# A four-head graph attention layer with 0/1 masks: exact waits and a hinted loop, the normalisation on ScalarE, and the accumulator banks emptied one step later

## The reference, cut to what matters

```python
# x: 8192 x 256 f32; adj: 8192 x 8192 int32, 0 or 1, about 0.2% ones; W: 4 heads x 256 x 64; a: 4 x 128
xt  = einsum('ni,hio->hno', x, W)
src = einsum('hnf,hf->hn', xt, a[:, :64]);  dst = einsum('hnf,hf->hn', xt, a[:, 64:])
e   = leaky_relu(src[:, :, None] + dst[:, None, :], 0.2)
e   = where(adj > 0, e, -inf)
h   = einsum('hij,hjf->hif', softmax(e, axis=2), xt)
out = layernorm(x + h.transpose(1, 0, 2).reshape(n, 256))      # over the 256 features, eps 1e-5
```

## Time and profile before

| | |
|---|---|
| time, 3 runs | median 2429.58 us (2426.62 to 2431.9) |
| profiled execution | 2433.28 us; its span in the trace 2431.5 us |
| PE busy | 2128.5 us, 88% |
| DVE busy | 2161.1 us, 89% |
| ACT busy | 1993.6 us, 82% |
| POOL busy | 90.7 us, 4% |
| DMA | 470.18 MB, mean 193 GB/s |
| granted TensorE clock, mean | 0.949 |

### The profile page before, as it was taken

One profiled execution on the slowest core, in us unless ns is written; L12 is line 12 of the kernel. 1 busy time (PEld: TensorE's weight loads), 2 busy tenths in 40 slices (PEclk: granted clock), 3 DMA queues, 4 the chain that ended last, 5 costly groups with the idle time before them and its releaser, 6 DMA issues. The chain is left out here.

```text
span 2431.5 us, 79550 instructions
## 1 busy us (share of the span) xinstructions
PE 2128.5 (88%) x34180; PEld 2093.7 (86%) x34180; DVE 2161.1 (89%) x2398; ACT 1993.6 (82%) x1981; POOL 90.7 (4%) x72
## 2 busy tenths in 40 slices
PE   7604999999999899998999999998989999999996
PEld 6503989998999899998999999998989988999996
DVE  4597999999889999999999999989999998988776
ACT  2235889888888898888889888888888988899995
POOL 0062000000000000000000000000000000000000
PEclk9856999999999999999999999999999999999998
DMA  8648776666555666666656666656556566623220
GB/s 300 208 188 316 256 245 228 231 210 226 182 187 188 222 215 193 194 193 216 196 186 202 212 211 195 195 194 222 190 189 205 187 223 193 193 82 111 77 55 19
DMA packets 236613, 470.18 MB, mean 193 GB/s; under 512 B 14656, under 2 KB 23104, under 8 KB 236224
## 3 DMA queue, kind: packets, MB, share of 16 engines
q1 hardware_dynamic: 231600, 447.53, 56.3%
q0 software_dynamic: 4352, 16.78, 2.0%
q10 hardware_dynamic: 272, 0.13, 0.0%
HBM read 438.83 MB, written 25.56 MB: 191 GB/s over the span
## 5 line engine op out<-in xcount | busy, mean ns | idle before, releaser
L385 ACT ACTIVATE big<-big,d_all 128x1024 int8<-128x1024 f32 x1792 | 1889.5, 1137 | 164.9 <-PE acc L747 162.0
L747 PE MATMUL acc<-big 128*128 128x130 f16 x32768 | 1955.0, 222 | 40.2 <-DVE big L549 20.2
L747 PEld LDWEIGHTS acc<-big 128*128 128x128 fp8e5 x32768 | 1929.7, 99 | 55.0 <-issue 50.9
L543 DVE SCALAR_TENSOR_TENSOR big<-big,AT 128x1024 uint32<-128x1024 uint32 x512 | 626.5, 1224 | 157.5 <-ACT big L385 118.6
L549 DVE SCALAR_TENSOR_TENSOR big<-AT,big 128x1024 uint32<-128x1024 uint32 x512 | 624.3, 1219 | 26.2 <-DVE big L543 0.5
L712 PE MATMUL tp<-ident,nat 128*128 128x128 f32 x1024 | 165.4, 287 | 227.3 <-DVE nat L464 109.2
L712 PEld LDWEIGHTS tp<-ident,nat 128*128 128x128 f32 x1024 | 114.4, 146 | 235.5 <-issue 232.3
L535 DVE TENSOR_SCALAR big<-big,d_all 128x1024 uint8<-128x1024 f32 x256 | 190.2, 743 | 0.0
L464 DVE TENSOR_SCALAR nat<-raw 128x2048 fp8e4<-128x2048 int32 x128 | 176.3, 1381 | 6.8 <-DMA raw<-in_adj_dram 6.8
L466 DVE TENSOR_SCALAR nat<-raw 128x2048 uint8<-128x2048 int32 x128 | 177.0, 1383 | 0.0
L479 DVE SCALAR_TENSOR_TENSOR AT<-AT,tp 128x512 uint32<-128x512 uint32 x224 | 152.8, 682 | 0.2
(11 more groups left out here) (46 smaller groups left out, 342.8 us busy)
## 6 DMA issues: line engine op xcount, KB each, us to landing
raw<-in_adj_dram SPq DMA_DIRECT2D x256, 1024.0 KB, 6.2
big<-v_parts SPq DMA_DIRECT2D x512, 260.0 KB, 3.5
v_parts<-big SPq DMA_DIRECT2D x16, 1040.0 KB, 4.2
big<-s_rows SPq DMA_DIRECT2D x32, 512.0 KB, 4.7
AT<-in_x_dram SPq DMA_DIRECT2D x16, 512.0 KB, 4.0
big<-in_x_dram POOLq DMA_DIRECT2D x8, 1024.0 KB, 8.5
out_dram<-big POOLq DMA_DIRECT2D x8, 1024.0 KB, 6.9
big<-in_L_gnn_W_dram SPq DMA_DIRECT2D x2, 128.0 KB, 2.6
```

The source lines that it names most:

```text
L385: ins = nc.scalar.activation(sgn[:, g % NB, b, :], srow[:, h % 2, :], ACT.Sign, bias=dflat[:, r:r + 1], scale=-1.0)
L543: nc.vector.scalar_tensor_tensor(out=word(sgn, g % NB), in0=word(sgn, g % NB), scalar=EDGE[plane], in1=edges(g), op0=ALU.bitwise_and, op1= ...
L747: return nc.tensor.matmul(acc[:, k, o:o + 2 * VO], m[:, g % NB, b, t * P:(t + 1) * P], Vr[:, v:v + 2 * VO], start=opens, stop=False, skip_ ...
```

## The change

Five edits. (1) TensorE's two pass loops carry a hint for their closing branch. (2) ScalarE's `low` moves from behind step 1 to inside step 2: one part after the second, third and fourth block of signs each. VectorE's `high` of all three parts moves from step 1 (part 0 between the two mask operations, the others behind them) to behind step 2's `rest_of` and `convert`; weighing and the rest follow one step later each. (3) VectorE compares the block for the next odd step behind the masks of the step before it, instead of ahead of that step's own masks; `keep` stands between pos and neg. (4) The wait on `AT` counts only the merges into the step's own tile. (5) Normalisation goes to ScalarE, steps 12 to 15 of the first pass of a chunk, two row tiles each, and at the very end; GpSimd makes the shift that it needs, with two more small operations.

```diff
-            def signs(n, g, h):
-                act.wait_ge(sums_done, n + 1)
-                for b in range(scalar_blocks(g)):
...
+            def normalise(c, ts):
+                act.wait_ge(shift_done, 2 * c + 2)
+                for t in ts:
+                    nc.scalar.activation(y[:, t, :], y[:, t, :], ACT.Identity, bias=shift[:, t:t + 1],
+                                         scale=rstd[:, t:t + 1]).then_inc(norm_done, 1)
...
                     for g in range(NG):
-                        signs(p * NG + g, g, h)
-                        if g == 1 and not (first and h == 0):
-                            for part in range(3):
-                                low(p - 1, part)
+                        act.wait_ge(sums_done, p * NG + g + 1)
+                        for b in range(scalar_blocks(g)):
+                            ins = sign(g, h, b)
+                            if b == scalar_blocks(g) - 1:
+                                ins.then_inc(sgn_done, 1)
+                            if g == 2 and b > 0 and not (first and h == 0):
+                                low(p - 1, b - 1)
+                        if g in (12, 13, 14, 15) and h == 0 and not first:
+                            normalise(c - 1, (2 * g - 24, 2 * g - 23))
...
-                        if scalar_blocks(g) < B:
-                            compares(n, g, h)
+                        masks_of(n, g, plane, c * H * HALF + h * HALF + (g + 1) // 2, last[g])
+                        if g < NG - 1:
+                            if scalar_blocks(g + 1) < B:
+                                compares(n + 1, g + 1, h)
...
-                        if ended and g == 1:
-                            high(p, 0)
+                        if g == 2:
+                            rest_of(n, g, plane, last[g])
                         for k in made_at(first, s):
...
-                        rest_of(n, g, plane)
+                        if g != 2:
+                            rest_of(n, g, plane, last[g])
                         if ended:
-                            if g == 1:
-                                high(p, 1)
-                                high(p, 2)
                             if g == 2:
+                                for part in range(3):
+                                    high(p, part)
+                            if g == 3:
                                 weigh(p, ec, eh)
...
-            with pe.Fori(H, NP - H) as p:
+            with nc.Fori(H, NP - H, engines=PE, hint_back_edge=True) as p:
                 one_pass(p, lambda g: [((p + H) * HALF + g // 2, g // 2)] if g % 2 == 0 else [])
-            with pe.Fori(NP - H, NP) as p:
+            with nc.Fori(NP - H, NP, engines=PE, hint_back_edge=True) as p:
                 one_pass(p, lambda g: [])
```

More of the change, by code:

```diff
@@ L17, in gat_residual_norm @@
     AX = mybir.AxisListType
+    PE = [mybir.EngineType.PE]
     RMAX = bass.bass_isa.ReduceOp.max
@@ L65, in gat_residual_norm @@
         half = sb("half", [P, T], fp32)
+        shift = sb("shift", [P, T], fp32)
         big = sb("big", [P, 24144], fp32)
@@ L147, in gat_residual_norm @@
         pow_done = sem("pow_done")
+        shift_done = sem("shift_done")
         norm_done = sem("norm_done")
@@ L326, in deviation @@
                 nc.gpsimd.tensor_tensor(out=rstd[:, :], in0=rstd[:, :], in1=half[:, :], op=ALU.pow).then_inc(pow_done, 1)
+                nc.gpsimd.tensor_scalar(shift[:, :], mv[:, :, 0], -1.0, None, ALU.mult).then_inc(shift_done, 1)
+                pool.wait_ge(pow_done, 2 * c + 2)
+                pool.wait_ge(shift_done, 2 * c + 1)
+                nc.gpsimd.tensor_tensor(out=shift[:, :], in0=shift[:, :], in1=rstd[:, :], op=ALU.mult).then_inc(shift_done, 1)
             def store(c):
@@ L379, in _, with sign @@
                     nc.scalar.activation(V_part(n, 2), rows_of(U2[n]), ACT.Copy, scale=1.0 / LOW).then_inc(hi_done, 1)
-            def signs(n, g, h):
-                act.wait_ge(sums_done, n + 1)
-                for b in range(scalar_blocks(g)):
[L384 to L387, removed]
+            def sign(g, h, b):
+                r = (g * B + b) * H + h
+                return nc.scalar.activation(sgn[:, g % NB, b, :], srow[:, h % 2, :], ACT.Sign,
+                                            bias=dflat[:, r:r + 1], scale=-1.0)
             def low(p, part):
@@ L418, in _ @@
                 low(NP - 1, part)
+            normalise(NC - 1, range(T))
         @block.vector
@@ L471, in keep @@
                 if not fresh:
-                    dve.wait_ge(neg_done, n - (g - u // 2 - 1) % NG + 4)
+                    z = (g - u // 2) % NG
+                    dve.wait_ge(pos_done if z == 0 else neg_done, n + 1 if z == 0 else n - z + 5)
                 to = AT[:, u // 2, :, u % 2, :]
@@ L544, in masks_of, with rest_of @@
                                                op0=ALU.bitwise_and, op1=ALU.bitwise_and).then_inc(pos_done, 1)
-            def rest_of(n, g, plane):
+            def rest_of(n, g, plane, kept):
+                dve.wait_ge(at_done, kept)
                 dve.wait_ge(sums_done, n + 1)
@@ L602, in spread @@
                 ins.then_inc(mv_done, 1)
[L604 to L608, removed]
             def chunk(c, plane, first=False, after_first=False, more=True):
-                kept = NG + 2 if first else UN * (c + 1) + 2 - sum(
-                    len(kept_at(False, after_first, z)) for z in range(3))
+                last = [UN * c + 2 * g + 4 for g in range(NG)]
                 for h in range(H):
@@ L626, in chunk @@
                                 keep(UN * (c + 1) + k, k + UN, plane, first, n, g)
-                                kept = kept + 1
+                                last[(k + UN) // 2] = UN * (c + 1) + k + 3
                             elif more:
                                 keep(UN * (c + 1) + k, k, 1 - plane, False, n, g)
-                                kept = kept + 1
-                        masks_of(n, g, plane, c * (NP // NC) * HALF + h * HALF + (g + 1) // 2 + 0, kept)
-                        if ended and g == 1:
-                            high(p, 0)
+                                last[k // 2] = UN * (c + 1) + k + 3
+                        if g == 2:
+                            rest_of(n, g, plane, last[g])
                         for k in made_at(first, s):
@@ L660, in chunk @@
                                 spread(c - 1)
[L661 to L664, removed]
             chunk(0, 0, first=True)
@@ L681, in _ @@
             spread(NC - 1)
-            normalise(NC - 1, range(T))
         @block.tensor
```

8 lines of the change are left out of this document (4 added, 4 removed).

## The result

The changed kernel takes 2542.05 us (median of 4 runs, 2541.64 to 2542.39) against 2428.1 us (4 runs, 2426.59 to 2431.9): ratio 1.0467, 95% interval 1.0449 to 1.0485. It is slower, as forecast, but by more: 2509 was forecast, with a range up to 2535. The profiled execution took 2542.08 us, its span 2540.5.

The account below looks back on a forecast made before the run. TensorE was bound by its closing-branch stops, with late banks behind. Ordinary passes +24.0, chunks' first passes +23.5, passes 1 to 3 +13.6, last four +16.8, end +2: +80 on 2433.3 gives 2513, as median 2509; range 2460 to 2535 us.

Parts of the forecast that it names:

- The banks: End of a pass: TensorE waits for the first `high`; an ordinary pass becomes 70.13 us, +1.41, 17 passes +24.0.
- S(14): What step 2's signs wait for at a pass's end; all issued by TensorE at T - 3.64.
- T: The moment at which TensorE would issue the next pass without any stop; the forecast's times count from it, in us.
- The hint hidden: Closing branch of TensorE's pass loop: its stop, 4.80 us, hinted or not, is hidden in the wait for the banks.
- Rival B: Pass ends: banks free as early as now, T + 2.78, with the branch gone; 2354 us; chance 0.12.
- VectorE's relief: VectorE's pass gets shorter; worth nothing where banks hold TensorE, but the 2.7 us of a chunk's first passes go.
- Passes 1 to 3: Early passes: 71.2 us each after, +2.6 for each of two; with pass 1, +13.6 together.
- Normalisation on ScalarE: First pass of a chunk: 4.0 us work plus 2.4 us wait make ScalarE 5.1 us late; 75.2 us a pass; +23.5.
- S(6): Step 6's counterpart of S(14); the shift was estimated to end some 14.2 us after it is done.
- lateness: How late ScalarE comes to step 2's signs in a chunk's first pass: 5.1 us, bounds 2.5 to 8.6.
- rival C: Pass ends: the longer stop costs more clock, 0.3 us by slope, 0.9 at worst, over 30 ends; 2536 us; chance 0.08.
- Rival A: Banks as forecast but ScalarE not late: shift ready, normalisations find room, 7 x 5 us go; 2474 us; chance 0.24.

Follow-up runs that it names:

- Experiment 7: Changed kernel with the three high parts ahead of step 2's conversion instead of behind it: 2500.88 us, ratio 1.0274.
- Experiment 4: Changed kernel with the low and high parts (emptying the banks) back in step 1, as in the kernel before: 2366.88 us, ratio 0.9728.
- Experiment 1: Changed kernel with TensorE's two pass loops unhinted, as before; all else stays: 2536.67 us, ratio 1.0426.
- experiment 2: Kernel before with nothing but the hint on TensorE's two pass loops: 2363.71 us, ratio 0.9709.
- 9: The kernel of experiment 8 with TensorE's two pass loops unhinted: 2394.3 us, ratio 0.9842.
- experiment 8: Changed kernel with the banks emptied in step 1 and normalisation on VectorE, both as before; hint, exact waits and early compares stay: 2314.51 us, ratio 0.9504.
- Experiment 5: Changed kernel with the negated mean (L330) made by VectorE instead of GpSimd: 2515.17 us, ratio 1.0326.
- Experiment 6: Changed kernel with ScalarE's normalisation in steps 14 and 15, four row tiles each, instead of steps 12 to 15: 2499.28 us, ratio 1.0262.

## Why the prediction was right in direction and too small

*The banks: right.* The chain from S(14) to the first `high` was forecast to let TensorE start at T + 6.65 and is at T + 6.45. An ordinary pass was forecast at 70.13 us and is 70.06. Experiment 7 takes one link out of the chain and gets its length back at the ends. Experiment 4 removes the delay, and the 175 us show how much the banks cost against a kernel in which they hold TensorE at almost no ordinary end. Against the kernel before it is far less, because its 4.64 us stop hid most of it.

*The hint hidden: right.* Experiment 1 shows it worthless in the changed kernel; experiments 2 and 9 show it worth 68 and 80 us where the banks are free in time. Rival B (the banks free as early as before) describes experiment 2: 2354, of which 16 are VectorE's relief, which that kernel doesn't have, so 2370; measured 2364, with restarts at T + 2.3 in most ordinary passes.

*VectorE's relief worth nothing there: in accord with the waits, not tested alone.* VectorE waits 320.9 us for signs. Where the banks are free in time, the relief shows: experiment 8 is 49 us under the hint alone. The three edits in it (early compares, `keep` between the masks, exact waits) were not taken apart.

*Passes 1 to 3: right.* 71.2 forecast; 372.35, 443.26 and 514.74 are the restarts, 70.9 and 71.5 apart.

*Normalisation on ScalarE: this term failed.* The step reads: "GpSimd adds 2.23 and two small operations." and, from it, "I estimate a wait of 2.4 us (0 to 3.6)." The wait is 6.92. The places were right: GpSimd starts 12.2 us after S(6) is done (2006.27 against 1994.1), where the forecast had about 11.5, and ScalarE is through at the same moment, where it had 11.9. The eight operations were right too (4.0 forecast, 4.04 measured; 588 ns one). Wrong was the price of GpSimd's operations. I took them at what they cost at the kernel's end, from the earlier trace rows, where VectorE is idle. In the middle VectorE works without a pause, and four operations take 6.9 us: 2.92 for the one that takes 0.25 alone. Experiment 5 removes it, and 27 us go. The kernel before already had a small sign of it: its L324 takes 0.53 us in the middle (at 1930.07) and 0.24 at the end.

In this pass L327, L330 and L333 each end within 0.11 us behind the end of a VectorE instruction (L560, L482, L567), so they look held by it. The Trainium skill, "SBUF — State Buffer", section "Who interferes with whom", states that a GpSimd instruction that reads SBUF and a VectorE instruction with two SBUF inputs, or one in a two-port mode, exclude each other for a whole instruction; these ends agree with it. Two things it doesn't settle here: L330 started beside L560 and lasted through two more of VectorE's instructions, the compare and the conversion, and the reciprocal root took its 1.68 us beside L567 and L560 as it does alone. No run varied what VectorE does beside GpSimd, so the cause behind the longer operations is argued, not shown.

*What that did to the sum.* With 6.92 for the wait, the forecast's own sum gives a lateness of 21.84 + 4.04 + 6.92 - 23.16 = 9.6 us in place of 5.1. The first passes of a chunk took 79.9 us on average instead of 75.2: 28 us more for passes 4, 8, ... 24, and 2.7 more for pass 28, where the forecast had no wait and 3.25 us came. For the profiled execution 2513 was forecast and 2542.1 measured, so these two make up the 29 us, with small differences between the other terms. The other 4 of the 33 us are no mechanism: 3.7 were taken off because the profiled execution of the kernel before lay above its median, and that of the changed kernel doesn't. The bound of 3.6 on the wait was too tight, and with it the range. (Its "2.5 to 8.6 us" of lateness also leaves out the 1.3 us of room that the 5.1 takes off.)

*Two readings beside it.* The five first passes of before, from the restarts of TensorE, took 71.05 to 71.95 us, 358.1 in all, and the other 17 took 68.67; the 357.2 and 68.72 of the prediction change nothing in its sum. And rival C's slope of clock against the length of a stop rests on two rows, where a third, in the earlier trace rows, has 7.74 us behind a stop of 2.24.

*The normalisation's place.* Rival A (ScalarE not late) would have been 2474. Experiment 6 shows 2499 nearly without the wait: the work alone makes a first pass 3 to 4 us longer. The prediction's reason against A, that ScalarE's idle time lies ahead of step 2, isn't what the trace shows. ScalarE is idle 21% of the span, but over a quarter of that lies in the set-up (142.6 us of the first 210), and in an ordinary pass the long stretch, 8.05 us, lies ahead of step 4, behind the bank work. From there to the next step 2 it has 0.33 us in 7.72. That is too little for the normalisation in steps 12 to 15.

## What to carry to other kernels

A stop can hide a second one behind it, and what a removal brings is their difference: ask first what is ready how long after the stop. Work that frees a resource belongs ahead of work that waits for that resource's user; here one step's delay put step 2's four signs, its two masks, a compare and a conversion ahead of the first `high`. And GpSimd's small operations are to be priced where they will run, beside a busy VectorE, not where VectorE is idle.

## What the runs showed of the hardware that was not expected

GpSimd's additions and multiplications on 128x8 elements took 0.20 to 0.25 us with VectorE idle. Beside its unbroken stream in the changed kernel they took 0.96 to 2.93 us (0.78 once, in pass 28), in experiment 4 one of them 4.08 in three chunks of six, and in experiment 6 once 5.23; in experiments 4 and 5 some kept their 0.20 to 0.24. The reciprocal root took 1.68 at the end and in most chunks, 2.71 in pass 28, and 2.52 in two chunks of experiment 5.

What a stop of TensorE costs in clock couldn't be read off its length. The first pair of steps behind it, 7.44 us at the full clock, took 7.74 after stops of 1.7 us (experiment 2), 7.74 and 9.11 after 2.24 and 2.18 (the kernel before), 9.11 at most ends after 4.56 (experiment 7), about 9.1 and about 10.2 by turns after 5.8, and 8.8 to 9.4 after 8.95 (both the changed kernel). Why, stays open.
